# Four slots for the probabilities, and PV for two chunks of keys at a time

## The chip, the cores and the metric

The program runs on one core of a Trainium2 chip. The metric is the time of one execution on the device in microseconds; smaller is better.

## The reference

Two transformer layers work on x of 8 batches, 512 tokens and 128 channels, everything in float32. Only the two attention stages matter here. With 16 heads of 8 channels each, layer 0 computes rotary q and k (one k and one v head shared by all), a causal softmax and the output projection; layer 1 has l2-normed q and k, a temperature for each head and no mask:

```python
att = jnp.einsum('bthd,bThd->bhtT', q, k) / math.sqrt(HD)
att = jnp.where(causal, -jnp.inf, att)          # layer 0 only
att = jax.nn.softmax(att, axis=-1)
out = jnp.einsum('bhtT,bThd->bthd', att, v).reshape(Bx, Tx, Cx)
return out @ Wo + bo
```

Around them stand a mixture of experts in layer 0 and a windowed attention with a feed-forward part in layer 1, which the change doesn't touch.

## The kernel before

`attend` runs once for each layer. The work is cut into units: one batch (8 of them) and four heads (UNITS = 4 units in a batch, UH = 4 heads), so 32 units in a layer. A unit has 16 tiles, one for each chunk k of 128 keys or queries (CH = 4) and each head h. They are called t0 to t15 below, with t = 4k + h. Five engines each run an order written out by hand, and they meet at semaphores.

Scores are made twice. An a tile (`a_tile`, L713) makes scores with queries on the partitions, from which VectorE takes row maxima (`maxima`, L910); a b tile (`b_tile`, L737) makes them with keys on the partitions and the maximum already subtracted (it comes in through three extra rows of Q), and ScalarE turns them into probabilities (`exp`, L825). While unit q has its b tiles, the a tiles of unit q + 2 run between them: the order on TensorE is a, b, a, b. The a tiles go through three PSUM banks (SA), so a tile waits for the maximum of three tiles before; at the first tile of each group of four units, which falls on the third unit of a batch (q = 2), it waits for all maxima so far. The b tiles go through two banks (SB), so a b tile waits for the exp of two tiles before. In layer 0 the tiles are causal: a tiles of chunk k are 128(k+1) columns wide, b tiles 512 - 128k, and each is followed by a 128-column matmul that adds the mask (L716, L740).

Between the tiles TensorE does five kinds of other work, in float32:

- `turn_max` (L726), after t1: transposes the maxima of unit q + 1. ScalarE copies the result twice (`negate` after exp t1, `first_part` after exp t2), GpSimd splits it in three parts (L871 to L878), SyncE stores it and loads it into Q (`move_max`, L667 and L669) for the b tiles of unit q + 1.
- `out_project` (L781), after t3; `turn_sums` (L763), after t8 = (2, 0); `spread_inverses` (L771), after t11 = (2, 3). VectorE's answer to the second is `invert_sums` after its maximum of t9, and to the third `normalise` (L924) after its maximum of t13.
- `pv` (L751), PV for one chunk of keys: four matmuls, one for each head, each into its own 32 columns of the array and partitions of bank OB. Each float32 matmul shows as two passes, so one `pv` is eight matmuls in the trace. `pv` of chunk k stands after tile (k+1, 1): after t5, t9 and t13 for chunks 0 to 2, and after t1 of the next unit for chunk 3. In layer 0 it is 512, 384, 256 and 128 columns wide.

`copy_out` (L841) on ScalarE, after exp t3 of the next unit, moves the sums out of OB; `pv` of chunk 0 waits for it. The probabilities have two slots (`g.probs[:, k % 2, ...]`), so that the first exp of a chunk waits for the `pv` of two chunks before. SyncE's `load` of unit q + 3 waits until all four `pv` of unit q - 1 are through, and `move_max` is queued behind it.

Of the kernel before, what the change touches and what calls it, by code (L numbers as in the profile page):

```python
# [12 lines left out]
ACT = mybir.ActivationFunctionType  # L13
AX = mybir.AxisListType

P = 128
B, N, C = 8, 512, 128
# [3 lines left out]
UH = H // UNITS  # L21
CH = N // P
# [542 lines left out]
def setup_attention(g):  # L565
    nc = g.nc
    g.Q = g.sb("Q", [RM, UNITS, UH, N], BF16)
    g.K = g.sb("K", [RM, UNITS, UH, N], BF16)
    g.V = g.sb("V", [P, UNITS, CH, UH * VW])
    g.wo = g.sb("wo", [P, 2, UNITS, C])  # L570
    g.bo = g.sb("bo", [P, 2])
    g.M = g.sb("M", [P, 2, CH, UH])
    g.mneg = g.sb("mneg", [UH, N])
    g.mres = g.sb("mres", [UH, N])
    g.mparts = g.sb("mparts", [UH, PARTS, N], BF16)
    g.probs = g.sb("probs", [P, 2, UH, N])
    g.osum = g.sb("osum", [P, N])
    g.rsum = g.sb("rsum", [P, CH * UH])
    g.rspread = g.sb("rspread", [P, CH * UH, VW])
    g.onorm = g.sb("onorm", [P, N])  # L580
    g.xres = g.sb("xres", [P, N])
    g.ytmp = g.sb("ytmp", [P, N])
    g.xnew = g.sb("xnew", [P, N])
    g.as_ = {n: g.sem("a_" + n) for n in (
        "setup", "a_scores", "a_max", "max_turned", "mneg", "mres", "mpart2", "mpart3", "m_stored",
        "m_loaded", "b_scores", "exp", "pv", "o_copied", "sums", "rsum", "rspread", "spread", "onorm", "yacc", "x_loaded", "ytmp", "xnew",
        "x_stored")}
    g.loaded = [g.sem(f"a_loaded{i}") for i in range(UNITS)]
    g.attention_setups += 1
    n_setup = g.attention_setups  # L590
    with nc.Block() as block:
        @block.sync
        def _(sp):
            sp.dma_start(g.wo[:, :, :, :], g.ins["wo"]).then_inc(g.as_["setup"], 16)
            sp.dma_start(g.bo[:, :], g.ins["bo"]).then_inc(g.as_["setup"], 16)
            sp.wait_ge(g.as_["setup"], 32 * n_setup)

        @block.gpsimd
        def _(pool):

            pool.memset(g.K[64:RM, :, :, :], 1.0)


def attend(g, layer, x, x_out):
# [10 lines left out]
    nc, s = g.nc, g.as_  # L615
    causal = layer == 0
    lo, hi = B * layer, B * (layer + 1)
    per = CH * UH
    scale = float(D) ** -0.5 if causal else 1.0
    SA, SB, OB, MB, YB = g.bank[0:3], g.bank[3:5], g.bank[5], g.bank[6], g.bank[7]  # L620
# [3 lines left out]
    def first_query(k):  # L624
        return P * k if causal else 0

    def batches(engine, batch):

        batch(lo, True, False)
        with engine.Fori(lo + 1, hi - 1) as i:  # L630
            batch(i, False, False)
        batch(hi - 1, False, True)

    def a_unit(q, last):
        return q + 2 if not (last and q >= 2) else None

    def m_unit(q, first, last):

        return q + 1 if not (first and q == 0) and not (last and q == UNITS - 1) else None

    with nc.Block() as block:
# [58 lines left out]
        def _(pe):  # L700
            def a_tile(i, u, k, h):

                n = u * per + k * UH + h
                slot, ring = u % UNITS, n % (UNITS * per)
                out = SA[ring % 3]
                width = P * (k + 1) if causal else N
                if k + h == 0:
                    pe.wait_ge(g.loaded[slot], (i + u // UNITS) * LOADS + LOADS)
                if ring >= 3:
                    pe.wait_ge(s["a_max"], i * 64 + n - 2)  # L710
                elif ring == 0 and (u or lo):
                    pe.wait_ge(s["a_max"], i * 64 + n)
                mm = pe.matmul(out[:, 0:width], g.Q[0:RK, slot, h, k * P:(k + 1) * P],  # L713
                               g.K[0:RK, slot, hk(h), 0:width], start=True, stop=not causal)
                if causal:
                    mm = pe.matmul(out[:, width - P:width], g.identb[:, :], g.mask[:, 0, :], start=False, stop=True)  # L716
                mm.then_inc(s["a_scores"], 1)
# [25 lines left out]
            def pv(i, q, k):  # L743

                t0 = first_query(k)
                slot = q % UNITS
                pe.wait_ge(s["exp"], i * 64 + q * per + (k + 1) * UH)
                if k == 0:
                    pe.wait_ge(s["o_copied"], i * 4 + q)
                for h in range(UH):  # L750
                    mm = pe.matmul(OB[VW * h:VW * (h + 1), t0:N], g.V[:, slot, k, VW * h:VW * (h + 1)],  # L751
                                   g.probs[:, k % 2, h, t0:N], start=(k == 0), stop=(k == CH - 1),
                                   skip_group_check=True)
                mm.then_inc(s["pv"], 1)

# [28 lines left out]
            def batch(i, first, last):  # L784
                for q in range(UNITS):
                    u, m = a_unit(q, last), m_unit(q, first, last)
                    for k in range(CH):
                        for h in range(UH):
                            if u is not None:
                                a_tile(i, u, k, h)  # L790
                            b_tile(i, q, k, h)
                            if (k, h) == (0, 1) and m is not None:
                                turn_max(i, m)
                            if h == 1 and k:
                                pv(i, q, k - 1)
                            elif h == 1 and not (first and q == 0):
                                pv(i, q - 1, CH - 1)
                            if (k, h) == (0, 3) and not (first and q < 2):
                                out_project(i, q - 2)
                            if (k, h) == (2, 0) and not (first and q == 0):  # L800
                                turn_sums(i, q - 1, m)
                            if (k, h) == (2, 3) and not (first and q == 0):
                                spread_inverses(i, q - 1)
# [4 lines left out]
                        a_tile(lo, u, k, h)  # L808
                turn_max(lo, u)
            batches(pe, batch)  # L810
            pv(hi, -1, CH - 1)
            out_project(hi, -2)
            turn_sums(hi, -1, None)
            spread_inverses(hi, -1)
# [2 lines left out]
        @block.scalar  # L817
        def _(act):
            def exp(i, q, k, h):
                n = q * per + k * UH + h  # L820
                t0 = first_query(k)
                if h == 0 and (q * CH + k >= 2 or not isinstance(i, int) or i):
                    act.wait_ge(s["pv"], i * 16 + q * CH + k - 1)
                act.wait_ge(s["b_scores"], i * 64 + n + 1)
                act.activation(g.probs[:, k % 2, h, t0:N], SB[n % 2][:, t0:N], ACT.Exp, scale=scale)\  # L825
                   .then_inc(s["exp"], 1)

            def negate(i, u):
                act.wait_ge(s["max_turned"], i * 4 + u + 1)
                act.wait_ge(s["mpart3"], i * 4 + u)  # L830
                act.activation(g.mneg[:, :], MB[0:UH, :], ACT.Copy, scale=-1.0).then_inc(s["mneg"], 1)

            def first_part(i, u):
                act.wait_ge(s["max_turned"], i * 4 + u + 1)
                act.wait_ge(s["m_stored"], (i * 4 + u) * 16)
                act.activation(g.mparts[:, 0, :], MB[0:UH, :], ACT.Copy, scale=-1.0).then_inc(s["mneg"], 1)  # L836

            def copy_out(i, q):
                act.wait_ge(s["pv"], i * 16 + 4 * q + 4)
                act.wait_ge(s["onorm"], i * 4 + q)  # L840
                act.activation(g.osum[:, :], OB[:, :], ACT.Copy).then_inc(s["o_copied"], 1)  # L841

            def batch(i, first, last):
                for q in range(UNITS):
                    m = m_unit(q, first, last)
                    for k in range(CH):
                        for h in range(UH):
                            exp(i, q, k, h)
                            if not (first and q == 0):
                                if (k, h) == (0, 3):  # L850
                                    copy_out(i, q - 1)
                            if m is not None:
                                if (k, h) == (0, 1):
                                    negate(i, m)
                                if (k, h) == (0, 2):
                                    first_part(i, m)

            for u in range(2):
                negate(lo, u)
                first_part(lo, u)  # L860
            batches(act, batch)
            copy_out(hi, -1)
# [1344 lines left out]
```

## Time and profile before

| | |
|---|---|
| median of 3 runs | 2899.45 us (2896.48 to 2900.97) |
| profiled execution, span from the first to the last instruction | 2897.5 us |
| busy: TensorE matmul / weight load | 81% / 47% |
| busy: VectorE / ScalarE / GpSimd | 57% / 47% / 37% |
| attention stage of layer 0 | about 180 to 640 us |
| attention stage of layer 1 | about 1195 to 1690 us |

The profiled execution's own time is its span, and the median of the runs is 2 us above it. Engines: PE is TensorE's matmuls, PEld its weight loads, DVE VectorE, ACT ScalarE, POOL GpSimd, SP SyncE. In the timeline the start of a row is the time from the span's start; matmuls overlap their neighbours, since a matmul's length includes the time to run out of the array, so what a matmul costs is read from one start to the next, not from its length.

### The profile page before, as it was taken

The numbers are of one execution on the slowest core, as the hardware profiler recorded it, in microseconds if no ns is written. First come the engines' busy times: TensorE is split into PE (matmuls) and PEld (weight loads), VectorE is DVE, ScalarE is ACT, GpSimd is POOL, SyncE is SP. The second block draws the span as 40 slices with busy tenths as digits, with TensorE's granted clock in tenths as the row PEclk, the third lists the DMA queues.
The fourth block names the chain that finished last, engine by engine and source line by source line (L and its number), as shares of the span: only waits on it lengthen the run. The fifth ranks groups of instructions, "written<-read, shape, count | busy, mean of one in ns | idle before, by whom it ended". The sixth has DMA issues, their size and how long they took to land. (4 is left out here: it accounts for less than half of the span.)

```text
span 2897.5 us, 48906 instructions
## 1 busy us (share of the span) xinstructions
PE 2349.5 (81%) x14180; PEld 1351.3 (47%) x14180; DVE 1664.4 (57%) x3472; ACT 1357.3 (47%) x3122; POOL 1072.3 (37%) x920
## 2 busy tenths in 40 slices
PE   4649999987084555799999975999999999999996
PEld 2325555545063343233333342655555555555553
DVE  3536666633112333577777624777777777777772
ACT  1125555540031111366666622666666666666662
POOL 2322222221404333122222214656555656555550
PEclk9759999995597666699999966999999999999997
DMA  3321211211133232222222111000000000000000
GB/s 96 125 89 53 66 53 53 64 34 60 52 89 97 79 87 82 69 71 69 62 62 67 52 51 73 16 11 11 11 11 11 16 15 15 15 15 21 14 12 11
DMA packets 114492, 141.81 MB, mean 49 GB/s; under 512 B 15712, under 2 KB 76899, under 8 KB 114144
## 3 DMA queue, kind: packets, MB, share of 16 engines
q1 hardware_dynamic: 112352, 136.53, 15.9%
q0 software_dynamic: 2048, 4.16, 0.6%
q8 instruction: 45, 0.74, 0.1%
q14 instruction: 47, 0.39, 0.0%
HBM read 90.60 MB, written 50.07 MB: 49 GB/s over the span
## 5 line engine op out<-in xcount | busy, mean ns | idle before, releaser
L910 DVE TENSOR_REDUCE M_sb<-bank 128x1 f32<-128x512 f32 (+3 forms) x1024 | 561.5, 586 | 327.0 <-PE bank L716 179.8
L825 ACT ACTIVATE probs_sb<-bank 128x512 f32<-128x512 f32 (+3 forms) x1024 | 496.5, 512 | 338.4 <-PE bank L740 164.6
L1764 ACT ACTIVATE l_p_sb<-bank,l_nb_sb,l_inv_sb 128x192 f32<-128x192 f32 x512 | 257.4, 507 | 368.5 <-DVE l_nb_sb L1948 367.0
L713 PE MATMUL bank<-K_sb,Q_sb 72*128 72x512 bf16 (+3 forms) x1024 | 363.1, 358 | 80.1 <-DMA V_sb<-v_dram 63.1
L737 PE MATMUL bank<-Q_sb,K_sb 75*128 75x512 bf16 (+3 forms) x1024 | 350.4, 345 | 7.3 <-ACT probs_sb L825 4.2
L871 POOL TENSOR_TENSOR mres_sb<-mneg_sb,mparts_sb 4x512 f32<-4x512 f32 x64 | 73.2, 1144 | 713.4 <-ACT mparts_sb L836 713.4
L1859 POOL TENSOR_TENSOR l_pn_sb<-l_p_sb,l_rs_sb 128x384 f32<-128x384 f32 x256 | 231.1, 903 | 182.0 <-DVE l_rs_sb L1954 158.8
L1834 POOL TENSOR_TENSOR l_ts_sb<-l_t_sb 128x512 f32<-128x512 f32 x128 | 162.2, 1267 | 283.4 <-DVE l_t_sb L1903 227.8
L713 PEld LDWEIGHTS bank<-K_sb,Q_sb 72*128 72x128 bf16 x1024 | 106.5, 104 | 333.0 <-DVE M_sb L910 205.2
L1943 DVE TENSOR_REDUCE l_mx_sb<-bank 128x2 f32<-128x384 f32 x256 | 141.9, 554 | 191.2 <-PE bank L1633 188.2
L1631 PE MATMUL bank<-l_kr_sb,l_qr_sb 128*128 128x192 f32 x1024 | 242.5, 339 | 0.0
L751 PE MATMUL bank<-probs_sb,V_sb 128*32 128x512 f32 (+3 forms) x2048 | 234.4, 529 | 6.1 <-ACT probs_sb L825 1.4
L1842 POOL TENSOR_TENSOR l_inv_sb<-l_clip_sb,l_minus_half_sb 128x8 f32<-128x8 f32 x128 | 225.0, 1759 | 0.0
L1631 PEld LDWEIGHTS bank<-l_kr_sb,l_qr_sb 128*128 128x128 f32 x1024 | 168.0, 194 | 83.2 <-issue 56.1
L1654 PEld LDWEIGHTS bank<-l_pt_sb,l_vt_sb 128*64 128x64 f32 x1792 | 96.7, 140 | 168.8 <-issue 111.6
L1641 PE MATMUL bank<-ident_sb,l_pn_sb 128*128 128x128 f32 x1024 | 172.3, 292 | 1.7 <-POOL l_pn_sb L1859 1.7
L1654 PE MATMUL bank<-l_pt_sb,l_vt_sb 128*64 128x128 f32 x1792 | 159.8, 295 | 13.5 <-ACT l_pt_sb L1773 11.4
L231 PE MATMUL bank<-x_norm_sb,mean_w_sb 128*128 128x512 f32 x64 | 63.0, 1085 | 123.1 <-DMA x_norm_sb<-x 78.1
L1773 ACT ACTIVATE l_pt_sb<-bank 128x512 f32<-128x512 f32 x256 | 152.3, 595 | 21.5 <-PE bank L1641 17.9
L1587 PE MATMUL bank<-lw_sb,l_xs_sb 128*128 128x512 f32 x256 | 137.2, 620 | 29.8 <-DMA l_xs_sb<-hx 22.8
L737 PEld LDWEIGHTS bank<-Q_sb,K_sb 75*128 75x128 bf16 x1024 | 100.4, 99 | 125.8 <-ACT probs_sb L825 64.4
L246 ACT ACTIVATE sq_sb<-xc_norm_sb 128x512 f32<-128x512 f32 x32 | 20.1, 627 | 263.1 <-DVE xc_norm_sb L239 263.1
(209 smaller groups left out, 4399.3 us busy)
## 6 DMA issues: line engine op xcount, KB each, us to landing
Q_sb<-qk_dram SPq DMA_DIRECT2D x576, 32.0 KB
v_dram<-vpad_sb SPq DMA_DIRECT2D x16, 1024.0 KB, 8.5
V_sb<-v_dram SPq DMA_DIRECT2D x64, 256.0 KB
qk_dram<-parts_sb SPq DMA_DIRECT2D x96, 128.0 KB
K_sb<-qk_dram SPq DMA_DIRECT2D x96, 96.0 KB
x_norm_sb<-x SPq DMA_DIRECT2D x24, 256.0 KB, 2.7
x<-xnew_sb SPq DMA_DIRECT2D x16, 256.0 KB, 2.1
ew_sb<-in_ew SPq DMA_DIRECT2D x16, 256.0 KB, 3.1
```

The lines of the kernel that those rows point to most:

```text
L713: mm = pe.matmul(out[:, 0:width], g.Q[0:RK, slot, h, k * P:(k + 1) * P], g.K[0:RK, slot, hk(h), 0:width], start=True, stop=not causal)
L737: mm = pe.matmul(SB[n % 2][:, t0:N], g.K[0:RM, q, hk(h), k * P:(k + 1) * P], g.Q[0:RM, q, h, t0:N], start=True, stop=not causal)
L751: mm = pe.matmul(OB[VW * h:VW * (h + 1), t0:N], g.V[:, slot, k, VW * h:VW * (h + 1)], g.probs[:, k % 2, h, t0:N], start=(k == 0), stop=(k ...
L825: act.activation(g.probs[:, k % 2, h, t0:N], SB[n % 2][:, t0:N], ACT.Exp, scale=scale)\
L910: dve.reduce_max(g.M[:, u % 2, k, h:h + 1], SA[ring % 3][:, 0:width], AX.X).then_inc(s["a_max"], 1)
L1631: pe.matmul(out, g.qr[:, e, p, t * P:(t + 1) * P], g.kr[:, p, t * P:t * P + WIN], start=True, stop=False, skip_group_check=True)
L1641: mm = pe.transpose(TB[:, j * P:(j + 1) * P], g.pn[:, n % 2, j // 2, (j % 2) * P:(j % 2 + 1) * P], g.ident[:, :])
L1654: mm = pe.matmul(OB[HD * e:HD * (e + 1), p * P:(p + 1) * P], g.vt[:, t - 1 + j, at:at + HD], g.pt[:, n % 2, 2 * e + j, :], start=(j == 1), ...
L1764: last = act.activation(g.pe_[:, n % 2, e, :], S[n % 2][:, WIN * e:WIN * (e + 1)], ACT.Exp, bias=g.lnb[:, n % 4, e:e + 1], scale=g.linv[:, ...
L1834: pool.tensor_tensor(g.lts[:, w, :, :], g.lt1[:, :, :], g.lt2[:, :, :], ALU.add).then_inc(s["tsum"], 1)
L1842: pool.tensor_tensor(g.linv[:, w, a % CH, :], g.lclip[:, w, :], g.minus_half[:, :], ALU.pow)\
L1859: pool.tensor_tensor(g.pn[:, n % 2, :, W:2 * P], g.pe_[:, n % 2, :, :], g.lrs[:, n % 4, :].unsqueeze(2).broadcast_to([P, 2, WIN]), ALU.mult)\
```

## The change

The probabilities get four slots, one for each chunk. `pv` of chunks 0 and 1 are both issued after tile (2, 1) = t9, and `pv` of chunks 2 and 3 both after t1 of the next unit (before: after t5, t9, t13 and the next t1). The first exp of a chunk now waits for the `pv` of four chunks before. The number of instructions and what they compute stay the same. The diff:

```diff
-    g.probs = g.sb("probs", [P, 2, UH, N])
+    g.probs = g.sb("probs", [P, CH, UH, N])
...
                     mm = pe.matmul(OB[VW * h:VW * (h + 1), t0:N], g.V[:, slot, k, VW * h:VW * (h + 1)],
-                                   g.probs[:, k % 2, h, t0:N], start=(k == 0), stop=(k == CH - 1),
+                                   g.probs[:, k, h, t0:N], start=(k == 0), stop=(k == CH - 1),
...
-                            if h == 1 and k:
-                                pv(i, q, k - 1)
-                            elif h == 1 and not (first and q == 0):
-                                pv(i, q - 1, CH - 1)
+                            if (k, h) == (2, 1):
+                                pv(i, q, 0)
+                                pv(i, q, 1)
+                            if (k, h) == (0, 1) and not (first and q == 0):
+                                pv(i, q - 1, 2)
+                                pv(i, q - 1, 3)
...
-            pv(hi, -1, CH - 1)
+            pv(hi, -1, 2)
+            pv(hi, -1, 3)
...
-                if h == 0 and (q * CH + k >= 2 or not isinstance(i, int) or i):
-                    act.wait_ge(s["pv"], i * 16 + q * CH + k - 1)
+                if h == 0 and (q or not isinstance(i, int) or i):
+                    act.wait_ge(s["pv"], i * 16 + q * CH + k - 3)
...
-                act.activation(g.probs[:, k % 2, h, t0:N], SB[n % 2][:, t0:N], ACT.Exp, scale=scale)\
+                act.activation(g.probs[:, k, h, t0:N], SB[n % 2][:, t0:N], ACT.Exp, scale=scale)\
```

## Rows read from the trace of the kernel before

**Rows 1.** Busy time in the middle of each attention stage; columns as the first line.
```profile
core 0: us, PE busy (x) PEld busy (x) DVE busy (x) ACT busy (x) POOL busy (x), PEclk, DMA share, GB/s
220.00:620.00 400.00, 382.86 (x3427) 218.74 (x3419) 248.79 (x552) 233.45 (x554) 109.27 (x96) 1.00 0.20 54
1220.00:1610.00 390.00, 381.88 (x2214) 152.87 (x2210) 298.34 (x496) 257.71 (x487) 94.03 (x83) 1.00 0.24 67
```

**Rows 2.** Timeline, TensorE, layer 1; start us, length us, engine, line, operation.
```profile
1407.81 0.38 PE L713 MATMUL bank<-K_sb,Q_sb 72*128 72x512 bf16 x1
...
1412.43 0.60 PE L726 MATMUL bank<-ident_sb,M_sb 128*4 128x128 f32 x4
...
1413.95 0.39 PE L713 MATMUL bank<-K_sb,Q_sb 72*128 72x512 bf16 x1
...
1414.84 1.02 PE L781 MATMUL bank<-onorm_sb,wo_sb 128*128 128x512 f32 x2
1415.70 0.38 PE L713 MATMUL bank<-K_sb,Q_sb 72*128 72x512 bf16 x1
...
1416.35 0.38 PE L737 MATMUL bank<-Q_sb,K_sb 75*128 75x512 bf16 x1
1416.76 1.06 PE L751 MATMUL bank<-probs_sb,V_sb 128*32 128x512 f32 x8
...
1419.06 0.39 PE L737 MATMUL bank<-Q_sb,K_sb 75*128 75x512 bf16 x1
...
1420.37 0.38 PE L737 MATMUL bank<-Q_sb,K_sb 75*128 75x512 bf16 x1
...
1421.68 0.39 PE L713 MATMUL bank<-K_sb,Q_sb 72*128 72x512 bf16 x1
...
1423.45 0.38 PE L713 MATMUL bank<-K_sb,Q_sb 72*128 72x512 bf16 x1
...
1427.46 0.60 PE L726 MATMUL bank<-ident_sb,M_sb 128*4 128x128 f32 x4
1427.99 1.07 PE L751 MATMUL bank<-probs_sb,V_sb 128*32 128x512 f32 x8
1428.98 0.39 PE L713 MATMUL bank<-K_sb,Q_sb 72*128 72x512 bf16 x1
```

**Rows 3.** Timeline, VectorE, layer 1, from t12 of a unit on.
```profile
1423.87 1.29 DVE L910 TENSOR_REDUCE M_sb<-bank 128x1 f32<-128x512 f32 x2 [0.48 <-PE bank L713]
1425.08 0.68 DVE L924 TENSOR_TENSOR onorm_sb<-osum_sb,bank 128x512 f32<-128x512 f32 x1
```

**Rows 4.** Timeline, ScalarE, layer 1, exp of t2 and `first_part` behind it.
```profile
1414.60 0.60 ACT L825 ACTIVATE probs_sb<-bank 128x512 f32<-128x512 f32 x1 [0.87 <-PE bank L737]
1415.09 0.57 ACT L836 ACTIVATE mparts_sb<-bank 4x512 bf16<-4x512 f32 x1
```

**Rows 5.** Timeline, TensorE, layer 0.
```profile
313.21 0.23 PE L713 MATMUL bank<-K_sb,Q_sb 72*128 72x128 bf16 x1
...
320.49 0.34 PE L713 MATMUL bank<-K_sb,Q_sb 72*128 72x384 bf16 x1
...
322.23 0.38 PE L713 MATMUL bank<-K_sb,Q_sb 72*128 72x512 bf16 x1
...
325.84 0.60 PE L726 MATMUL bank<-ident_sb,M_sb 128*4 128x128 f32 x4
326.37 0.42 PE L751 MATMUL bank<-probs_sb,V_sb 128*32 128x128 f32 x8
326.73 0.23 PE L713 MATMUL bank<-K_sb,Q_sb 72*128 72x128 bf16 x1
```

**Rows 6.** Timeline, TensorE, windowed attention: PV with two and with one chunk.
```profile
1912.83 0.66 PE L1654 MATMUL bank<-l_pt_sb,l_vt_sb 128*64 128x128 f32 x8
...
1925.14 0.44 PE L1654 MATMUL bank<-l_pt_sb,l_vt_sb 128*64 128x128 f32 x4
```

**Rows 7.** Timeline, SyncE, layer 0: `move_max` of the unit that follows.
```profile
332.44 0.32 SPq L667 DMA_DIRECT2D m_dram<-mparts_sb  x1
334.85 0.26 SPq L669 DMA_DIRECT2D Q_sb<-m_dram  x1
```

## The prediction

> **What bounds the kernel now.** I read first the busy time by stretch, then the timeline of one unit on each engine. In the middle of both attention stages TensorE is busy 96 to 98% of the time at full clock (granted clock 1.00, the 2.4 GHz level), VectorE 62 and 76%, ScalarE 58 and 66% [rows 1]. That looks like a stage in which everything taken off TensorE comes back. But a busy share is an average, and a unit isn't even: TensorE's side works (turn_max, out_project, turn_sums, spread_inverses, four pv) lie between runs of a and b tiles. In such a run a tile pair costs TensorE 0.44 us (two tiles from 1413.95 to 1414.84) [rows 2], while VectorE needs 0.61 us for each maximum (two in 1.29, the last 0.68 long) [rows 3] and ScalarE 0.49 for each exp [rows 4]. Both followers are slower than TensorE in a run and catch up while it does side work, as far as the three banks of a tiles and the two of b tiles let them. So what matters is where the side work stands, and the change moves just that.
>
> **What it saves on TensorE.** From b of t9 to a of t10, with pv between, it takes 1.31 us (1420.37 to 1421.68); b alone takes 0.22, so pv costs 1.09 [rows 2]. Its streaming: the eight matmuls take 1.06 at 512 columns [rows 2] and 0.42 at 128 [rows 5], so 0.21 per 128 columns, 0.85 for 512. Thus 0.24 us of each pv is getting in and out. With two pv in one go one such 0.24 may fall away: twice in a unit, 128 times in all. Second, pv of chunk 0 stands after t5, where copy_out is just at work: from b of t5 it takes 0.41 to pv (1416.35 to 1416.76) [rows 2], 0.09 more than after t9, where it is 0.32 (the 1.31 less the 0.99 that a pv takes from its first matmul on, 1427.99 to 1428.98) [rows 2]. This wait goes, since copy_out is long done at t9. The four slots by themselves give nothing: the exp waits for a pv that was issued three tiles before it, and the exp in the rows starts on the b tile instead [rows 4]. They only make the new order possible.
>
> **What it costs, layer 1.** I roll one unit forward in three parts, each set against the rows.
>
> Part A, from a of t12 to a of t2 of the next unit: now 5.53 us (1423.45 to 1428.98) [rows 2]. There pv of chunk 2 after t13 gave VectorE 1.09 us to catch up, and its normalise (0.68 long) sits right there. In the new order six tile pairs run without a break: t12 to t15, t0 and t1. VectorE starts the maximum of t12 0.42 after the part's start, t13 at 1.02, normalise at 1.63 [rows 3]; then, at about 0.60 each, t14 at 2.23 and t15 at 2.83, done at 3.51. TensorE alone would be at a of t1 at 2.2 and at turn_max at 2.6. But a of t1 waits for the maximum of t14 (2.91), and turn_max, which needs all 16 maxima of its unit, waits for t15: it starts at 3.56, against 4.01 now (1427.46). Then turn_max 0.53, pv of chunk 2 0.85 and of chunk 3 0.99 [rows 2]: 5.93. So A grows by 0.40 us. Of the 1.09 that leaves the stretch only 0.45 comes back, and the 0.85 of streaming are paid behind turn_max, where nothing needs them.
>
> In the third unit of each batch a of t0 already waits for all maxima. Now turn_max starts 4.62 after a of t12 there (1407.81 to 1412.43) [rows 2]; then it would be 3.56 plus two tile pairs (0.87), 4.43, and A grows by 0.66.
>
> Part B, from a of t2 to a of t10: now 7.73 (1413.95 to 1421.68) [rows 2]. Two pairs and out_project bring a of t4 to 1.75. ScalarE starts exp of t2 at 0.65 (as 1414.60 against 1413.95) and has to do exp t2, first_part, exp t3, copy_out, exp t4 in a row: exp t4 at 2.58, done at 3.15 [rows 4]. b of t6 waits for it, 3.20, where TensorE alone would be at 2.85; before, pv of chunk 0 after t5 covered this. From there exp sets the pace: exp t6 starts at 3.62 and b of t8 follows at 4.27. Then as now 1.31 to b of t9 (1419.06 to 1420.37) and 1.31 to a of t10, with 0.85 more for the second pv: 7.74. Both savings are eaten by b tiles that wait for exp; B stays as it is.
>
> Part C, t10 to t12, is unchanged (1.77, cover and order are the same).
>
> Sum for layer 1: the last two units have no a tiles, and there I take nothing. 22.5 units at 0.40 and 7.5 at 0.66: 14.0 us.
>
> **Layer 0.** Tiles are narrower, VectorE's maxima of t12 to t15 are all 512 wide. By the same roll, with 0.06 more for the mask matmul, the maximum of t15 is done at 3.57 and turn_max starts at 3.62, now at 3.61 (322.23 to 325.84) [rows 5]: nothing at all comes back, and the 256 columns of pv of chunk 2 (0.43) are added behind it. Part A goes from 4.50 (322.23 to 326.73) [rows 5] to 4.94, and by nearly the same, 0.43, in the third unit. Part B, now 7.28 (313.21 to 320.49) [rows 5], has the same block of ScalarE, with exp t4 only 384 wide; the roll gives about 7.20. Sum 0.36 a unit, 30 units: 10.8 us.
>
> **The seam between the two pv.** So far the second pv costs its streaming alone. No row shows two pv back to back. The nearest are in the windowed attention, where PV of two chunks takes 0.66 us for eight matmuls and of one chunk 0.44 for four [rows 6]: the second pair of instructions adds 0.22 for two passes of 128 columns, of which 0.21 is streaming. So the seam is 0.01 there, with two column groups of 64 where pv has four of 32. The other end is the full 0.24, if the array empties between the two. I take 0.04, near the low end because that row is the same kind of matmul into the same two halves again: 128 seams, 5 us. Both ends stay in the range (1 to 31 us). The Trainium skill, in "TensorE: Matmul & The Clock Gate", on what happens when you issue a matmul, says that weight loads are pulled ahead of running matmuls if they go to the background buffer; that would put the seam at zero, and rows 6 agree.
>
> **Sum.** 14.0 + 10.8 + 5 = 30 us on the span of 2897.5, which gives 2927.5; the median of the runs stands 2 us above that span, so 2929.5 us.
>
> **What is moved past the queues.** The last pv of a unit ends later by the streaming of chunk 2 (0.85, or 0.43 in layer 0). Behind it on SyncE wait the 13 loads of unit q + 3 and then move_max. In layer 0 move_max issues its second DMA at 334.85 and the first had come back after 2.41 [rows 7]; if the second takes as long it is there at 337.3. The b tile that needs it is t0 of the next unit. It stands two tile pairs and a wait, some 1.2 us, ahead of a turn_max that comes one unit of 13.52 (313.21 to 326.73) after the one at 325.84 [rows 5], so at 338.1. A margin of 0.9 less 0.4 stays, and layer 1 units are 1.5 us longer. On ScalarE copy_out is queued behind exp t3 and ahead of exp t4; its pv is through before exp t2 can start, so nothing waits. I cost both at nothing.
>
> **Rivals.**
>
> *The saving on TensorE lands in full: faster.* This decides if VectorE and ScalarE keep up, that is, if turn_max starts by 2.6 in part A. Then 128 times 0.24, 31 us, and the wait for copy_out, about 0.10 in layer 1 and up to 0.2 in layer 0, 9 us at most: 2860 us. For it speaks 96 to 98% busy [rows 1]; against it the lengths of the maxima [rows 3], five of which with normalise don't fit into six tile pairs. The Trainium skill, in "TensorEngine Tiling (Array Packing)", Key Properties, says that changing the tiling mode drains TensorE, and the change halves the number of changes; the 0.24 us agree with it. By that rule alone the kernel gets faster, as in this rival. 10%.
>
> *The array empties at the seam.* Nothing is saved by the merge while all waits are added: 25 + 31 = 56 us, 2955. 12%.
>
> *Savings and waits cancel*, within 6 us of 2899: the waits would have to be half of what I worked out, for instance if pauses of a few tenths that I don't see move into the new ones. 5%.
>
> *move_max comes late.* If its second DMA takes 1 us longer than the first, b of t0 waits in layer 0 and the sum grows by some 0.5 us in 32 units, 16 us: 2945. 5%.
>
> *The forecast*, seam below 0.1: 68%.
>
> **How the numbers follow.** An error of 0.1 us in either part of a unit is 6 us, so the forecast's own range is 2915 to 2945. To leave out no more than the faster rival and most of the case without change, and to take in the empty seam, the range is 2912 to 2957. A change of 0.2% (6 us) is about what a measurement of this kernel can tell from none. Faster by over 0.2%: 0.10. Within: 0.05. Slower: 0.85.
>
> **What would show it.** In the profile after: turn_max starts some 3.6 us after a of t12 in layer 1, with a of t1 and turn_max released by VectorE's maxima (L910); b of t6 released by exp (L825), with a pause of about 0.35; units of 15.4 to 15.5 us in layer 1 against 15.03, and of 13.9 against 13.52 in layer 0; 16 matmuls of L751 in one row, some 1.95 us long. It is wrong if turn_max comes right behind b of t1, if a of t10 comes well before 7.7 after a of t2, or if b of t0 waits for a DMA.

## The result and the profile after

The changed kernel takes 2974.8 us (median of 4 runs, 2971.1 to 2975.4), the kernel before 2898.1: 1.026 times as long (95% interval 1.024 to 1.029), 77 us more where 30 were forecast. The profiled execution has a span of 2973.5. All of it comes from the two attention stages. From the first to the last `copy_out` of a stage, layer 0 takes 438.1 us (416.7 before) and layer 1 526.1 (462.5). The rest of the span is 9 us shorter; the time between the two stages varied from 569 to 589 us over all the profiles below, although its code is the same in all, so that part says nothing about the change.

The page of the changed kernel: busy time and, in 40 slices, the clock that TensorE was granted.

```profile
span 2973.5 us, 48916 instructions
...
PE 2386.5 (80%) x14180; PEld 1359.2 (46%) x14180; DVE 1658.4 (56%) x3472; ACT 1363.2 (46%) x3122; POOL 1072.6 (36%) x920
...
PEclk9869999996596665699899875999999999999997
```

And the busy time in a stretch of each attention stage (columns as in [rows 1]; the granted clock stands behind the POOL column):

```profile
240.00:560.00 320.00, 295.15 (x2621) 174.16 (x2614) 190.09 (x425) 178.03 (x420) 81.12 (x71) 0.97 0.19 55
1260.00:1660.00 400.00, 382.24 (x2012) 147.20 (x2014) 267.82 (x452) 240.09 (x446) 85.74 (x75) 0.92 0.21 58
```

TensorE is nearly as busy as before (92% in layer 0 and 96% in layer 1, where [rows 1] have 96 and 98%) and does clearly less in the time: 2012 matmuls in the 400 us of layer 1, where the kernel before has 2265 in the same stretch. Part of the reason is in the clock: 0.92, where [rows 1] have 1.00. In both attention stages of the kernel before it doesn't fall once. (A fall is here a step of the granted clock from 1.00 to 0.50.)

So two units have to be read, one in which the clock stays up and one in which it doesn't. First one at full clock, TensorE, layer 1:

```profile
1558.60 0.39 PE L713 MATMUL bank<-K_sb,Q_sb 72*128 72x512 bf16 x1
...
1561.22 0.38 PE L713 MATMUL bank<-K_sb,Q_sb 72*128 72x512 bf16 x1
1561.80 0.39 PE L737 MATMUL bank<-Q_sb,K_sb 75*128 75x512 bf16 x1 [0.20 <-ACT probs_sb L828]
...
1562.50 0.38 PE L713 MATMUL bank<-K_sb,Q_sb 72*128 72x512 bf16 x1
1562.88 0.39 PE L737 MATMUL bank<-Q_sb,K_sb 75*128 75x512 bf16 x1
...
1564.19 0.38 PE L737 MATMUL bank<-Q_sb,K_sb 75*128 75x512 bf16 x1
1564.50 1.92 PE L751 MATMUL bank<-probs_sb,V_sb 128*32 128x512 f32 x16
1566.36 0.39 PE L713 MATMUL bank<-K_sb,Q_sb 72*128 72x512 bf16 x1
...
1568.13 0.38 PE L713 MATMUL bank<-K_sb,Q_sb 72*128 72x512 bf16 x1
...
1571.09 0.39 PE L713 MATMUL bank<-K_sb,Q_sb 72*128 72x512 bf16 x1 [0.20 <-DVE M_sb L913]
...
1571.69 0.60 PE L726 MATMUL bank<-ident_sb,M_sb 128*4 128x128 f32 x4
1572.22 1.92 PE L751 MATMUL bank<-probs_sb,V_sb 128*32 128x512 f32 x16
1574.08 0.39 PE L713 MATMUL bank<-K_sb,Q_sb 72*128 72x512 bf16 x1
```

b of t6 waits for exp (1561.80), and a of t1 for VectorE's maximum (1571.09), as forecast. Part B begins with a of t2 (1558.60): b of t6 starts 3.20 us later and a of t10 7.76, where 3.20 and 7.74 were forecast. An a tile costs 0.22 us, so TensorE pauses 0.36 us at b of t6 (1561.22 to 1561.80) and 0.16 at b of t8 (1562.50 to 1562.88). Part A, from a of t12 (1568.13): turn_max after 3.56 us, a of the next t2 after 5.95, where 3.56 and 5.93 were forecast and [rows 2] have 4.01 and 5.53. Two pv in one go are 16 matmuls in 1.92 us, against 1.07 for eight.

Then the length of a unit, from `copy_out` to `copy_out` on ScalarE; the first two rows frame the unit above, the last two a later one:

```profile
1560.70 0.57 ACT L844 ACTIVATE osum_sb<-bank 128x512 f32<-128x512 f32 x1
...
1576.17 0.57 ACT L844 ACTIVATE osum_sb<-bank 128x512 f32<-128x512 f32 x1
...
1697.78 0.57 ACT L844 ACTIVATE osum_sb<-bank 128x512 f32<-128x512 f32 x1
...
1714.84 0.57 ACT L844 ACTIVATE osum_sb<-bank 128x512 f32<-128x512 f32 x1
```

15.47 us and 17.06. What lies in the longer one, by the timeline of TensorE and by two stretches:

```profile
1698.88 0.39 PE L737 MATMUL bank<-Q_sb,K_sb 75*128 75x512 bf16 x1 [0.20 <-ACT probs_sb L828]
...
1701.53 3.46 PE L751 MATMUL bank<-probs_sb,V_sb 128*32 128x512 f32 x16
1704.92 0.50 PE L713 MATMUL bank<-K_sb,Q_sb 72*128 72x512 bf16 x1
```

```profile
1698.00:1701.40 3.40, 3.20 (x19) 1.49 (x17) 2.93 (x5) 2.99 (x6) 2.88 (x3) 1.00 0.53 145
1702.00:1704.90 2.90, 2.90 (x16) 0.44 (x8) 0.70 (x3) 0.23 (x1) 0.00 (x0) 0.50 0.17 45
```

After t4 to t8, a run without pv and with the pause for exp, the granted clock goes from 1.00 to 0.50 (2.4 to 1.2 GHz), just as the two pv start. They take 3.46 us instead of 1.92. In layer 1 the clock falls 27 times, mostly at this place, and 20 of the 31 lengths from `copy_out` to `copy_out` are 17.06 us or more. In layer 0 it falls once in a batch, in the third unit, behind the wait for all maxima:

```profile
403.50 0.23 PE L713 MATMUL bank<-K_sb,Q_sb 72*128 72x128 bf16 x1 [1.83 <-DVE M_sb L913]
...
404.30 0.66 PE L726 MATMUL bank<-ident_sb,M_sb 128*4 128x128 f32 x4
404.89 1.51 PE L751 MATMUL bank<-probs_sb,V_sb 128*32 128x256 f32 x16
```

```profile
400.00:404.70 4.70, 2.87 (x29) 1.79 (x26) 3.67 (x7) 1.71 (x6) 0.00 (x0) 1.00 0.01 2
404.90:408.00 3.10, 3.10 (x26) 1.71 (x26) 0.58 (x2) 1.45 (x4) 0.00 (x0) 0.50 0.06 16
```

### The profile page after: what moved, and what is told of

Read it like the earlier page. It is cut to its first block and busy times, and to the rows that moved or that the text cites. A ratio compares the mean times of both kernels' runs of the same rounds, so it can differ in the third digit from the quotient of the medians.

```text
span 2973.5 us, 48916 instructions
## 1 busy us (share of the span) xinstructions
PE 2386.5 (80%) x14180; PEld 1359.2 (46%) x14180; DVE 1658.4 (56%) x3472; ACT 1363.2 (46%) x3122; POOL 1072.6 (36%) x920
## 5 line engine op out<-in xcount | busy, mean ns | idle before, releaser
L737 PE MATMUL bank<-Q_sb,K_sb 75*128 75x512 bf16 (+3 forms) x1024 | 360.9, 354 | 20.3 <-ACT probs_sb L828 17.5
L751 PE MATMUL bank<-probs_sb,V_sb 128*32 128x512 f32 (+3 forms) x2048 | 249.8, 614 | 0.0
L1776 ACT ACTIVATE l_pt_sb<-bank 128x512 f32<-128x512 f32 x256 | 152.3, 595 | 16.7 <-PE bank L1644 13.1
```

The source lines that it names most:

```text
L737: mm = pe.matmul(SB[n % 2][:, t0:N], g.K[0:RM, q, hk(h), k * P:(k + 1) * P], g.Q[0:RM, q, h, t0:N], start=True, stop=not causal)
```

## The experiments

Two theories about the falls stood against each other: that stretches without pv, in which TensorE pauses for exp or maxima, let the clock fall, or that two pv in one go do it. And the 0.4 us a unit at full clock were to be traced to VectorE. Each kernel ran beside the kernel before, whose median in the four groups was 2895.0, 2888.4, 2896.8 and 2899.6 us. Falls are counted in the profiled execution of each kernel, from the first to the last `copy_out` of a stage, for layer 0 and layer 1 in this order. In a diff with the last pv moved, the matching change behind the last unit is left out.

**The slots alone.** The changed kernel with `pv` put back:

```diff
-                            if (k, h) == (2, 1):
-                                pv(i, q, 0)
-                                pv(i, q, 1)
-                            if (k, h) == (0, 1) and not (first and q == 0):
-                                pv(i, q - 1, 2)
-                                pv(i, q - 1, 3)
+                            if (k, h) == (1, 1):
+                                pv(i, q, 0)
+                            if (k, h) == (2, 1):
+                                pv(i, q, 1)
+                            if (k, h) == (3, 1):
+                                pv(i, q, 2)
+                            if (k, h) == (0, 1) and not (first and q == 0):
+                                pv(i, q - 1, 3)
```

> The order of the kernel before (pv after t5, t9, t13 and the next t1) with the four slots and the new wait of exp. Theory (what costs is the order on TensorE: pauses in long runs of tiles, and falls of the granted clock behind them): 2899 us, granted clock in layer 1's attention 1.00, units of 13.5 and 15.0 us. Rival (the larger probabilities' buffer or the changed waits cost by themselves): above 2910 us.

2894.9 us against 2895.0, ratio 1.000 (0.999 to 1.001), no falls, units as before to 0.04 us. The rival, above 2910, is out. The slots and the changed wait cost nothing and bring nothing.

**Only the first two together.** This diff and those below are against the changed kernel, like the one above.

```diff
+                            if (k, h) == (3, 1):
+                                pv(i, q, 2)
                             if (k, h) == (0, 1) and not (first and q == 0):
-                                pv(i, q - 1, 2)
                                 pv(i, q - 1, 3)
```

> Only chunks 0 and 1 in one go after t9; chunk 2 after t13, chunk 3 after the next t1. Theory: part A (t12 to the next t2) is as before, part B (t2 to t10) has pauses at b of t6 and t8 and no pv from t2 to t9. At full clock that is nearly even, 2900 to 2905 us, units 13.55 and 15.05. If stretches without pv and with pauses let the clock fall, layer 1 still has units of about 17 us as in the changed kernel, where the fall comes some 8 us after turn_max, and the time is 2930 to 2955; layer 0 has no fall, as its falls came at turn_max, behind part A. Rival (only part A's wait for maxima matters): 2900 and no unit of 17 us.

2936.3 us, ratio 1.013 (1.011 to 1.016), 41 us more. Units without a fall are 13.49 and 15.06 us, against 13.52 and 15.03 before; units with one are mostly 16.6 to 16.7, third units 17.3. There are 3 and 19 falls (a text below says 18, which leaves out the one in the stage's first unit), where none was expected in layer 0; in layer 1 all but one come 6.7 to 7.8 us after turn_max. Two stretches side by side, before and at one of them:

```profile
1516.00:1523.00 7.00, 6.80 (x37) 2.79 (x34) 4.92 (x9) 5.58 (x11) 3.40 (x3) 1.00 0.28 80
1523.00:1526.20 3.20, 3.20 (x17) 0.59 (x16) 1.23 (x3) 0.60 (x1) 0.00 (x0) 0.50 0.32 96
```

**Only the last two together.**

```diff
+                            if (k, h) == (1, 1):
+                                pv(i, q, 0)
                             if (k, h) == (2, 1):
-                                pv(i, q, 0)
                                 pv(i, q, 1)
```

> Only chunks 2 and 3 in one go after the next t1; chunk 0 after t5, chunk 1 after t9. Theory: part A has the whole wait for maxima, so at full clock units are 13.9 in layer 0 and 15.4 to 15.5 in layer 1, with 28 us added in all: 2926. In part B pv after t5 keeps TensorE at work, so that falls some 8 us after turn_max are gone; falls at turn_max (layer 0, and the third unit of layer 1's batches) may stay: 2926 to 2945. Rival (two pv in one go let the clock fall by themselves): units of 17 us here too, with the fall at the pair behind turn_max, 2960 and more.

2940.5 us, ratio 1.015 (1.012 to 1.018). Units at full clock are 13.95 and 15.44 us, so the whole loss of part A is here. In layer 1 the falls 8 us after turn_max are gone; 5 stay, all in the third unit of a batch, and 7 in layer 0. TensorE, layer 1, a pair behind such a fall and one without:

```profile
1505.35 3.42 PE L751 MATMUL bank<-probs_sb,V_sb 128*32 128x512 f32 x16
...
1522.29 1.92 PE L751 MATMUL bank<-probs_sb,V_sb 128*32 128x512 f32 x16
```

A pair stands in all 32 units of this stage and falls come with 5, so the pair by itself isn't it.

**More work in the pauses.** The changed kernel, with the first matmul of five a tiles issued twice into the same bank:

```diff
+TWICE = (0, 1, 6, 7, 15)
...
+                if UH * k + h in TWICE:
+                    pe.matmul(out[:, 0:width], g.Q[0:RK, slot, h, k * P:(k + 1) * P],
+                              g.K[0:RK, slot, hk(h), 0:width], start=True, stop=True)
                 mm = pe.matmul(out[:, 0:width], g.Q[0:RK, slot, h, k * P:(k + 1) * P],
```

> The changed kernel with more work for TensorE and nothing else: the first matmul of the a tiles t0, t1, t6, t7 and t15 is issued twice into the same bank. These stand where TensorE waits for exp or for maxima; the 0.22 us each (0.06 to 0.22 in layer 0) mostly fill a wait, and add at most 0.1 us to a unit. Theory (the clock falls where a stretch without pv has pauses): the falls go or become few, units of 15.5 and 13.9 us, 2925 to 2940. Rival (the two pv in one go make the clock fall): the pairs are still there, so 2975 to 2985. Rival (the waits themselves are all of the loss): no gain either, 2975.

2960.6 us, ratio 1.021 (1.019 to 1.024): 14 us less than the changed kernel (11 when each is set against the kernel before of its own group), though TensorE does more, but 20 more than the upper end of what was expected. What was expected happened in part B: of the falls some 8 us after turn_max in layer 1 one is left, regular units are 15.54 us. But 7 falls in layer 0 and 9 in layer 1 stayed, nearly all behind the third unit's wait for all maxima; a doubled t0 stands behind that wait too and can't fill it.

**Still more.** With `EXTRA = {0: 1, 1: 1, 6: 1, 7: 1, 14: 1, 15: 2}` as the number of added matmuls for each tile.

> The changed kernel with still more work for TensorE in the stretches without pv: the first matmul of a tiles t0, t1, t6, t7 and t14 issued twice, that of t15 three times. With the doubled tiles of the run before, the falls of the clock in part B of layer 1 went and those at turn_max in the third unit of a batch (8 in layer 1, 7 in layer 0) stayed. Theory (the falls come behind a stretch in which TensorE had little to do, the third unit's wait for all maxima being the last such place): most of these go too; the added matmuls cost at most 0.2 us in a unit at full clock, units of 15.6 to 15.7 and 14.0 us: 2930 to 2945. Rival (the third unit's falls have to do with the pair of pv behind turn_max): they stay, 2960 to 2970.

2954.1 us, ratio 1.024 (1.020 to 1.028) to its own kernel before. 3 and 6 falls: of the seven third units of each layer, five in layer 0 and three in layer 1 are without a fall, where twice had one in all fourteen (seven in layer 1, not eight as the text above has it), so these falls too depend on what TensorE does ahead of turn_max. The time missed the expected range by 9 us, because the added matmuls cost 0.15 us in a unit (15.62) and 4 to 5 us ahead of the stage, where the same tiles run alone, and nine falls were left. Set against its own kernel before it is no faster than twice (66 us more in both): by time alone this run decides nothing.

**Only the first two together, two tiles doubled.** As pair_front, with `TWICE = (6, 7)`.

> As pair_front (chunks 0 and 1 in one go after t9, the rest as before), with the first matmul of the a tiles t6 and t7 issued twice, which is TensorE work where it pauses for exp, 32 us above the kernel before without them. Theory (pauses in the run without pv from t2 to t8 let the clock fall, and the falls are the loss of pair_front): the 18 falls of layer 1 go or nearly all of them, units of 15.1 us, and 30 us come back though TensorE does more: 2900 to 2908 against 2895 to 2897. Rival (two pv in one go behind t9 make it fall): 2936 to 2945.

2903.3 us, ratio 1.002 (1.001 to 1.004). Between the first and the last `copy_out` neither layer has a fall left; only layer 0 starts its first unit at 0.50 (19.02 us, in an execution that is 8 us above the median). The other units are 13.50 and 15.04 to 15.06, the third ones as before. The loss of pair_front shrinks from 41 us (not 32, as the text above has it) to 4. The stretch of layer 1, and the pair behind t9:

```profile
1260.00:1660.00 400.00, 394.23 (x2314) 165.06 (x2313) 304.79 (x508) 266.08 (x503) 99.32 (x88) 1.00 0.23 65
```

```profile
1508.93 1.92 PE L755 MATMUL bank<-probs_sb,V_sb 128*32 128x512 f32 x16
```

Same pair, same place, same length of a unit at full clock; 2 x 0.22 us of matmul in the pauses for exp, and the clock holds. So it is what TensorE does between t2 and t9 that makes it fall in part B, and not the pair.

**Half of each maximum.** In both kernels, for the base and for the change (each row maximum over half of the columns, the other half left out):

```diff
-                dve.reduce_max(g.M[:, u % 2, k, h:h + 1], SA[ring % 3][:, 0:width], AX.X).then_inc(s["a_max"], 1)
+                dve.reduce_max(g.M[:, u % 2, k, h:h + 1], SA[ring % 3][:, 0:width // 2], AX.X).then_inc(s["a_max"], 1)
```

> The kernel before, with each row maximum taken over half of the columns only (the other half is left out), which makes VectorE's 512-column maximum some 0.34 us instead of 0.60. It is the base for half_after. Theory: waits for maxima go, units of 12.8 to 12.9 us in layer 0 and 14.9 in layer 1, no falls: some 30 us under the kernel before.

> The changed kernel with each row maximum taken over half of the columns only (the other half is left out), against half_before. Theory (VectorE's maxima hold part A back): turn_max starts 3.0 to 3.1 us after a of t12 in layer 1 instead of 3.56, and at full clock a unit is only 0.1 us longer than in half_before in either layer (12.9 to 13.0 and 14.9 to 15.0). The pauses for exp at b of t6 and t8 stay, so falls of the clock in part B of layer 1 stay possible: half_after is 6 us above half_before at full clock, up to 45 with falls. Rival (the moved pv itself makes part A longer, whatever VectorE does): units at full clock are still 0.4 us longer than in half_before.

2870.9 and 2910.4 us. At full clock a unit is now 13.0 us in layer 0 and 15.02 in layer 1 in the changed order, and 13.0 and 15.00 in the order before: the 0.4 us of part A are gone. (half_before came out 26 us under the kernel before where 30 were expected, with 15.00 in layer 1 instead of 14.9.) TensorE, layer 1, from a of t12 to turn_max, 3.11 us:

```profile
1612.36 0.38 PE L713 MATMUL bank<-K_sb,Q_sb 72*128 72x512 bf16 x1
...
1615.47 0.60 PE L726 MATMUL bank<-ident_sb,M_sb 128*4 128x128 f32 x4
```

The falls in part B of layer 1 stay (19), since exp is as slow as ever, and with them most of the 40 us between the two kernels.

**Both causes away.** As half_after, with `TWICE = (6, 7)`.

> The changed kernel with both suspected causes taken away: maxima over half of the columns only (the other half is left out), and the first matmul of the a tiles t6 and t7 issued twice. To be set against half_before (2871). Theory: no waits for maxima to speak of and few falls, so the change costs 5 to 12 us here instead of 77: 2876 to 2883, units of 15.1 and 13.0 us. Rival (something else than VectorE's pace and the clock is left): above 2890.

2878.8 us, 8 above half_before (they ran in different groups; by the ratios to their kernels before, 0.992 and 0.990, it is 6). One fall in each stage is left, in the last two units. The change costs 6 to 8 us here, of 77.

**Another order with the same slots.** pv where the followers need time: chunk 0 after t9, chunks 1 and 2 after t15, chunk 3 after the next t2.

```diff
                             if (k, h) == (2, 1):
                                 pv(i, q, 0)
+                            if (k, h) == (3, 3):
                                 pv(i, q, 1)
-                            if (k, h) == (0, 1) and not (first and q == 0):
-                                pv(i, q - 1, 2)
+                                pv(i, q, 2)
+                            if (k, h) == (0, 2) and not (first and q == 0):
                                 pv(i, q - 1, 3)
```

> The four slots used to put pv where VectorE and ScalarE need time, not where it is done soonest: chunk 0 after t9, chunks 1 and 2 in one go after t15, chunk 3 after the next t2. By the same roll of the unit as in the prediction, at full clock a unit of layer 0 is 12.8 us (13.5 before) and one of layer 1 14.8 to 14.9 without the longer third unit (15.0 and 15.65 before): 40 us less at most, 25 by the full sums, so 2855 to 2870 against 2895. There is no pv from t3 to t9 and pauses of 0.2 us at b of t6 and t8, so falls of the clock as in pair_front may cost up to 35 of it: 2855 to 2905. Rival (two pv in one go are harmful wherever they stand): above 2900.

2882.1 us, ratio 0.998 (0.996 to 1.000). Units at full clock are 12.77 and 14.87, as rolled, with a pair in each. Layer 0's stage is 21 us shorter (395.8), layer 1's 13 longer (475.6), with 8 falls that last 44 us together: units with one take 16.0 to 18.1 us. They settle more than the time does, since the pair stands after t15 here and a single pv after t9. TensorE at t9 in layer 1, and the stretches on both sides of the fall:

```profile
1427.69 1.85 PE L751 MATMUL bank<-probs_sb,V_sb 128*32 128x512 f32 x8
```

```profile
1424.00:1427.70 3.70, 3.67 (x22) 1.68 (x20) 3.20 (x6) 2.88 (x6) 2.17 (x2) 1.00 0.40 115
1427.90:1431.00 3.10, 3.10 (x12) 0.71 (x5) 1.69 (x5) 0.95 (x2) 0.00 (x0) 0.50 0.40 120
```

All eight falls begin 6.0 to 7.5 us after turn_max, behind the pauses for exp and around t9, where only the single pv stands (1.85 us instead of 1.07). None comes at the pair: a fall doesn't need one.

The same with `TWICE = (5, 7)`:

> As the order with chunk 0 after t9, chunks 1 and 2 after t15 and chunk 3 after the next t2, with the first matmul of the a tiles t5 and t7 issued twice, to keep TensorE at work in the pauses at b of t6 and t8. Theory: no falls in layer 1, a cost below 0.1 us a unit, 2860 to 2875. If the order without the doubling has no falls, this one is 0 to 6 us slower than it.

2867.4 us, ratio 0.993 (0.990 to 0.995), the fastest of those that compute the same result, and faster than both kernels. Units of layer 1 are 14.93, the stage 460.7. Two falls are left in layer 1, in its last two units, and two in layer 0, in its first unit and in the last but one:

```profile
240.00:560.00 320.00, 316.32 (x2971) 194.17 (x2970) 213.34 (x476) 194.71 (x469) 89.38 (x79) 1.00 0.22 61
1260.00:1660.00 400.00, 394.07 (x2306) 165.36 (x2304) 286.14 (x477) 267.22 (x498) 92.72 (x81) 0.99 0.21 60
```

**Without any pair.** Chunk 0 after t5, 1 after t9, 2 after t15, 3 after the next t2:

> The order before with only two pv moved: chunk 2 after t15 (was t13) and chunk 3 after the next t2 (was t1); no two in one go. No stretch without pv is much longer than before, so no falls. The roll gives 13.3 and 14.8 to 14.85 us for a unit at full clock, 3 to 6 us less in all: 2888 to 2893 against 2895.

2877.9 us, ratio 0.996 (0.995 to 0.998), 10 us less than before instead of 3 to 6. No falls; units 13.1 to 13.6 and 14.91, the third ones 14.27 and 15.37 (14.32 and 15.65 before).

## Why the prediction was right and wrong

The sign, the mechanism and the sum at full clock were right; the time was wrong, because the sum took TensorE's clock for given.

- **The views.** Reading past the busy share was right: in layer 1 it is 96 to 99% in all orders, the good ones and the bad (in layer 0 it is 92 to 99%).
- **What it saves.** The time from b of t9 to a of t10 with two pv is 2.17 us (1564.19 to 1566.36), less 0.22 for b is 1.95; two single ones are 2 x 1.09. The saving is 0.23, forecast 0.24. The Trainium skill, in "TensorEngine Tiling (Array Packing)", Key Properties, says that a change of tiling mode drains TensorE. The trace agrees with it by this 0.23 us, and the time still went the other way.
- **The seam.** 16 matmuls take 1.92, eight 1.07: 0.85 more, as much as the prediction's estimate of the streaming. The seam is zero, where 0.04 was taken (5 us of the sum too many). The rival of the empty array is out.
- **Part A, layer 1.** 5.95 us, forecast 5.93, and half_after shows that VectorE's maxima are the cause, not only the releaser in a row.
- **Part B.** The pause at b of t6 was forecast, and its price at full clock, nothing, was right: pair_front's units without a fall are as long as before. But it was not free, because of the clock.
- **The units.** 15.47 us in layer 1 (15.44), 13.93 in layer 0 (13.88), and 16.36 in third units that had no fall. By these 22.5 x 0.44 + 7.5 x 0.71 = 15 us in layer 1, and some 22.5 x 0.41 + 7.5 x 0.5 = 13 in layer 0 (the 0.5 from the third units of 14.83 us in more): 28 us at full clock, forecast 25 without the seam.
- **What failed.** The first paragraph of the prediction says "at full clock (granted clock 1.00, the 2.4 GHz level)", and every price in the sum is one of that clock. That it stays at 1.00 was no step with bounds and no rival. Of the 85 us by which the two stages grew, 28 are the forecast's and the other 57 come with the falls (63.6 less 15 in layer 1, 21.4 less 13 in layer 0). The size fits: the clock stands at 0.50 for 123 us of the two stages, and half of that, 61 us, is the most that can be lost by it (in pair_front 82 us, and 41 were lost). An upper end of 2957 for all unknowns was too low because this one was not among them.
- **The queues.** move_max was no cause: no pause at b of t0 names a DMA, and half_twice leaves no room for it beyond 6 to 8 us.

The Trainium skill, in "TensorE: Matmul & The Clock Gate", A second HAM failure mode: psum-queue depth-cycling, tells of a kernel in which short idle times of TensorE between groups of matmuls make its clock go back and forth between half and full rate. This case's rows agree (1.00 and 0.50 in neighbouring stretches, behind pauses of some 0.35 and 0.15 us), and front_twice shows that matmuls put into the pauses end it.

What stays open: the unit at 1561 us has the same order and the same pauses ahead of its pair as the one at 1698, and its clock doesn't fall. The order makes the fall possible; which units get it, and why several in a row do, these runs don't show. Nor do they tell whether it is the pause for exp alone or, with it, turn_sums behind t8, whose matmuls have only four columns each.

## What to carry to other kernels

Where a busy engine feeds slower ones through a few buffers, its side work is also the time in which they catch up: side work that is moved away from a run of tiles can cost nearly its length again behind it, so roll one unit forward before merging anything to save switching. And count what TensorE does in the stretch that the change leaves bare: here 0.5 us of pauses (at b of t6 and b of t8) at a place that looked free cost up to 1.6 us a unit in the clock. With free slots it paid here to place work where the followers are behind (third_late 10 us less than before, late_twice 21 with its added matmuls), not where most of it is merged.

## What the runs showed of the hardware

- The granted clock went from 1.00 to 0.50 within an attention stage in which TensorE was 96% busy, at the start of a pair of pv that then took 3.46 us instead of 1.92. In pair_front two added matmuls of 0.22 us in each unit brought the number of falls in layer 1 from 19 to none and the time of the kernel from 2936 to 2903 us: more work, less time.
- Float32 matmuls into the same four column groups ran on with no gap that these rows show: 0.85 us for the second eight of 512 columns, and getting in and out (0.23 us) is paid once.
